# Attention and gated feed-forward on eight cores: f32 products replaced by f16 high and low parts, and two evacuations moved to ScalarE

## The reference, cut to what matters

```python
x = L0_attn_x                                  # (8, 2048, 1024) f32
xn = _layernorm(x, axis=-1)
qkv = einsum('bnd,ed->bne', xn, w_qkv)         # q, k, v of 512 columns each
sim = einsum('bid,bjd->bij', q, k) * 512**-0.5 # causal
s = einsum('bnd,od->bno', softmax(sim) @ v, w_out) + b_out
h = silu(xn @ (w_gate/127).T) * (xn @ (w_up/127).T)   # hidden 3072, weights are int32
g = silu(h @ (w_down/127).T)
return x + s * g
```

## Time and profile before

| | us |
|---|---|
| median of 3 runs | 3124.9 |
| the profiled execution | 3124.2 |
| its span on the slowest core | 3122.6 |
| PE busy | 2814.2 (90%) |
| DVE busy | 223.4 (7%) |
| ACT busy | 216.1 (7%) |
| spans of the eight cores | 3111.6 to 3122.6 |

### The profile page before, as it was taken

How to read it: one execution, slowest core, us unless ns; L and a number is a source line. 1 busy time by engine, 2 the same in 40 slices (tenths; PEclk the granted TensorE clock), 3 DMA queues, 4 the chain that set the end, 5 groups by cost and what they waited for, 6 DMA issues and landing times.

```text
span 3122.6 us, 17440 instructions; the slowest of 8 cores (3111.6 to 3122.6 us)
## 1 busy us (share of the span) xinstructions
PE 2814.2 (90%) x6812; PEld 1313.7 (42%) x6812; DVE 223.4 (7%) x356; ACT 216.1 (7%) x347; POOL 1.9 (0%) x7
## 2 busy tenths in 40 slices
PE   5668998564888899999999999999999999999997
PEld 4555444221434344444444444444444444444443
DVE  1111001000111000000010000001000001000001
ACT  2111001100111100000000000000000000000000
POOL 0000000000000000000000000000000000000000
PEclk9888998876999999999999999999999999999998
DMA  3000002997000032223232223223223223222222
GB/s 96 27 27 0 27 14 61 168 169 147 21 14 21 19 84 79 81 69 127 74 108 81 68 80 121 74 74 108 81 81 107 86 77 108 79 69 81 94 74 101
DMA packets 235905, 240.34 MB, mean 77 GB/s; under 512 B 6129, under 2 KB 211185, under 8 KB 235250
## 3 DMA queue, kind: packets, MB, share of 16 engines
q1 hardware_dynamic: 234674, 199.39, 21.2%
q0 software_dynamic: 624, 37.75, 7.2%
q10 hardware_dynamic: 528, 2.10, 0.2%
HBM read 222.43 MB, written 54.53 MB: 89 GB/s over the span
## 4 chain that ended last, share of the span: by engine, by line
PE 88%; another core or an unknown queue 4%; ACT 3%; issue 2%; DVE 1%; DMA 1%; DVEq 0%; ACTq 0%; SPq 0%
PE psA L246 58%; PE psA L896 11%; PE psB L246 9%; PE psC L896 5%; PE psB L896 5%; ACT oaT L678 1%; ACT xnT L440 1%; ACT xnsc L424 1%; ACT pT L629 0%; ACT oaf L661 0%; DVE st L402 0%; ACTq L959 0%; DVEq L404 0%; DMA xin<-x 0%
## 5 line engine op out<-in xcount | busy, mean ns | idle before, releaser
L246 PE MATMUL psA<-xnT,wgb 128*128 128x512 f32 x1536 | 681.6, 597 | 19.3 <-ACTq L959 10.0
L246 PE MATMUL psA<-xnT,wub 128*128 128x512 f32 x1536 | 674.9, 593 | 0.0
L246 PEld LDWEIGHTS psA<-xnT,wgb 128*128 128x128 f32 x1536 | 294.5, 192 | 391.4 <-issue 391.4
L246 PEld LDWEIGHTS psA<-xnT,wub 128*128 128x128 f32 x1536 | 292.5, 190 | 366.7 <-issue 366.7
L896 PE MATMUL psA<-wdb,hT 128*128 128x512 f32 x768 | 345.5, 593 | 5.7 <-DVEq L959 5.7
L246 PE MATMUL psA<-xnT,wqf 128*128 128x512 f32 x512 | 233.8, 621 | 22.7 <-ACTq L959 17.9
L246 PE MATMUL psB<-vtk,pT 128*128 128x512 f32 x272 | 133.7, 650 | 108.4 <-DVEq L959 96.0
L896 PEld LDWEIGHTS psA<-wdb,hT 128*128 128x128 f32 x768 | 145.9, 190 | 190.4 <-issue 190.4
L246 PE MATMUL psA<-wvf,xnT 128*128 128x256 f32 x512 | 140.6, 444 | 54.1 <-ACTq L959 54.1
L896 PE MATMUL psC<-wdb,hT 128*128 128x512 f32 x384 | 180.5, 592 | 0.0
L896 PE MATMUL psB<-wdb,hT 128*128 128x512 f32 x384 | 180.5, 593 | 0.0
(11 more groups left out here) (57 smaller groups left out, 417.0 us busy)
## 6 DMA issues: line engine op xcount, KB each, us to landing
wgb<-wgb_scr SPq DMA_DIRECT2D x96, 512.0 KB, 3.9
wub<-wub_scr SPq DMA_DIRECT2D x96, 512.0 KB, 5.2
wdb<-wdb_scr SPq DMA_DIRECT2D x96, 512.0 KB, 3.2
xt<-x SPq DMA_DIRECT2D x16, 512.0 KB, 3.5
sscr<-stl SPq DMA_DIRECT2D x16, 512.0 KB, 2.9
sin<-sscr SPq DMA_DIRECT2D x16, 512.0 KB, 7.6
xin<-x SPq DMA_DIRECT2D x16, 512.0 KB, 9.0
out<-otl SPq DMA_DIRECT2D x16, 512.0 KB, 3.5
```

Source lines behind the costliest of these rows:

```text
L246: k.op("te", lambda e, lf=lf, rf=rf, j=j, n=n, pf=psum_ap_fn: e.matmul(pf(), lf(), rf(), start=(j == 0), stop=(j == n - 1)), inc=(inc if j ...
```

## The change

Two things change.

1. `MODE` becomes "split". `xnT`, `qT`, `kT`, the V tiles, `pT`, `oaT` and `hT` are each held as two f16 tiles, high (the rounded value) and low (the rest). The weights of the projections and of the output are multiplied by 64 and split in the same way; the FFN weights are whole numbers up to 127 and need one f16 tile. A product of two split operands becomes three f16 matmuls (high x high, high x low, low x high): projections, scores, PV, output. A product with an FFN weight becomes two. Scratches and buffers of the FFN weights are f16, so POOL's three DMAs write f16 and the loads of wgb, wub and wdb carry 256 KB instead of 512 KB, in pieces of 256 B (gate, up) and 2 KB (down) instead of 512 B and 4 KB. New on DVE: `emit_wv_split` and `emit_wsplit` (multiply, then multiply and subtract), a subtraction behind each evacuation by ACT, and in the FFN three operations per slice (multiply, cast, subtract) instead of one. `wo` is loaded in four parts, each split by ACT and DVE before the next is loaded.

2. `emit_v_group` and `emit_qk_group` evacuate the high part on ACT (`activation`, Identity); DVE then computes the low part. Waits for the bank go by that last writer. The scores also wait for ACT's count at the end of stage 1.

The core of the diff (the V group; the q and k group has the same edit with 512 columns and `dst`, m, n):

```diff
-MODE = "fp32"
+MODE = "split"
...
         if prev is not None:
-            k.wait("te", "ve", prev)
+            k.wait("te", prev[0], prev[1])
...
-        k.wait("ve", "pe", pe_g)
+        k.wait("se", "pe", pe_g)
+        k.op("se", lambda e, tc=tc, hh=hh, bank=bank: e.activation(
+            vtk[0].ap()[:, tc, hh * 256:(hh + 1) * 256],
+            psA.ap()[:, bank * 512: bank * 512 + 256], AF.Identity, bias=zeroc.ap()))
+        k.drain_inc("se", "se")
+        se_c = k.cnt["se"]
         if split:
-            k.op("ve", lambda e, tc=tc, hh=hh, bank=bank: e.tensor_copy(
-                vtk[0].ap()[:, tc, hh * 256:(hh + 1) * 256],
-                psA.ap()[:, bank * 512: bank * 512 + 256]))
-            k.op("ve", lambda e: e.drain())
+            k.wait("ve", "se", se_c)
             k.op("ve", lambda e, tc=tc, hh=hh, bank=bank: e.tensor_tensor(
                 vtk[1].ap()[:, tc, hh * 256:(hh + 1) * 256],
                 psA.ap()[:, bank * 512: bank * 512 + 256],
                 vtk[0].ap()[:, tc, hh * 256:(hh + 1) * 256], ALU.subtract))
+            k.drain_inc("ve", "ve")
+            ve_evac_qk[bank] = ("ve", k.cnt["ve"])
         else:
-            k.op("ve", lambda e, tc=tc, hh=hh, bank=bank: e.tensor_copy(
-                vtk[0].ap()[:, tc, hh * 256:(hh + 1) * 256],
-                psA.ap()[:, bank * 512: bank * 512 + 256]))
-        k.drain_inc("ve", "ve")
-        ve_evac_qk[bank] = k.cnt["ve"]
+            ve_evac_qk[bank] = ("se", se_c)
...
     ve_p1_done = k.cnt["ve"]
+    se_p1_done = k.cnt["se"]
...
             k.wait("te", "ve", ve_p1_done)
+            k.wait("te", "se", se_p1_done)
```

More of the change, by code:

```diff
@@ L376, in emit_qk_group @@
         m = mi % 4
-        k.wait("ve", "pe", pe_g)
+        k.wait("se", "pe", pe_g)
+        k.op("se", lambda e, dst=dst, m=m, n=n, bank=bank: e.activation(
+            dst[0].ap()[:, m, n * 512:(n + 1) * 512],
+            psA.ap()[:, bank * 512:(bank + 1) * 512], AF.Identity, bias=zeroc.ap()))
+        k.drain_inc("se", "se")
+        se_c = k.cnt["se"]
         if split:
[L379 to L382, removed]
+            k.wait("ve", "se", se_c)
             k.op("ve", lambda e, dst=dst, m=m, n=n, bank=bank: e.tensor_tensor(
@@ L386, in emit_qk_group @@
                 dst[0].ap()[:, m, n * 512:(n + 1) * 512], ALU.subtract))
-        else:
[L388 to L392, removed]
+            k.drain_inc("ve", "ve")
+            ve_evac_qk[bank] = ("ve", k.cnt["ve"])
+        else:
+            ve_evac_qk[bank] = ("se", se_c)
     emit_wq_load(0)
```

## The result

The changed kernel takes 2091.1 us (median of 8 runs, 2088.3 to 2093.4) against 3125.9: a ratio of 0.6692, interval 0.6684 to 0.6700. The forecast was 2330 us with a range of 2050 to 2470; the measured time lies in the range, 239 us under the forecast and 16 us under the rival in which the clock stays at 1.00 (2107).

A forecast was written before the change was run, and what follows sets the result against it. PE was taken as the bound, with FFN streams two thirds of the span. At clock 0.81: 3124 - 743 (FFN) + 15 (seams) - 21 (first stage) - 2 (q, k) + 25 (wo) - 66 (attention) = 2332, said 2330 us; range 2050 to 2470.

The forecast's parts named there:

- the rival in which the clock stays at 1.00: FFN products run at full granted clock, 977 us less than before, total 2107 us; chance 0.27.
- What bounds the kernel: Whole kernel: PE is busy all the time in the feed-forward part, whose 4608 records take 1972 us, two thirds of the span.
- The price of a stream: FFN products: an f16 matmul of 512 columns takes 216 ns, so 4608 take 995 us at clock 1.00.
- The clock: FFN: granted clock taken as 0.81, so products take 1229 us, 743 less than now; chance 0.5 at or near 0.81.
- FFN seams: Before down phases and at h=2 of three slabs: new waits, sum +15 us at 0.81, +24 at 1.00.
- Weight feed: FFN weight loads: 4.25 us of DMA a step, landed 5.6 us after release, hidden under the step, so nothing.
- the feed rival: FFN weight loads: each 256 B piece costs as two and sets the step; 2490 us, or 2420 at clock 1.00; chance 0.06.
- First stage: V rounds gain nothing, three rounds with q and k gain 15 us, dense blocks 6: sum -21 us.
- q and k: Slices mi 2 to 7: faster products, but six waits of 4.5 us for the weight split; 166 against 168, -2 us.
- wo: Output weight before attention: four rounds of load, ACT and DVE at 6.5 us each, +25 us.
- Attention: Products -85 us, low-part chains +37, cold clock +16, shorter weight conversion -34: sum -66 us.
- the f16 stream at f32's price: All matmuls: 512 f16 columns take 428 ns like f32, FFN stays 1972 us, kernel about 3570 us; chance 0.02.

The follow-up runs named there:

- the experiment with one pass: Gate and up leave out the pass with the low part of xn, against the changed kernel: 1876.9 us profiled, 1880.9 and 2015.8 in the other two.

## Why the prediction was right where it was, and wrong where it was not

**What bounds the kernel.** Right. PE sets the end through 4608 FFN streams before and after, and the stages with three passes gained little.

**The price of a stream.** Right: 216 ns taken from the V record by equal bytes, 215 measured. That the bytes are the reason is not shown; the number was one row's, and it fitted.

**The clock.** This is the term that was mis-sized, and the step of the forecast that failed: "I take 0.81 for FFN". The runs show 1.00, in the changed kernel and with full-size operands in the place of the low parts and weights. It is a term of 995 / 0.81 - 995 = 234 us, and the forecast missed by 239. The row of 0.81 that it rested on is a mean over full and half clock after pauses of PE: of the same V products 32 took 10.01 us behind a pause and 7.07 without one. So it was a row on idle time, used for a stage that has almost none. The nearest row on dense work was the f32 FFN at 1.00, and the traces spoke for it alone. The rule of the Trainium skill that all-core dense matmul runs at 13/16 of the clock ("TensorE: Matmul & The Clock Gate", Part 1) was not borne out in these stretches: by it a stream would have taken some 265 ns (215 x 16/13, an estimate).

That the range of 2050 to 2470 holds 2091 is owed to its lower end, which was drawn for the full clock, a case given 0.27. The forecast itself stood on the other one.

**FFN seams.** Right in place and size: PE waits 2.7 us ahead of each down phase (10.8 in four) and waited 1.4 before (5.7 in four), so 1.3 more where 1.0 to 1.4 was put, and the new wait at h=2 of a slab, worked out from SP's order as 6 us, measured 6.4. The cast takes 0.43 us, inside its bounds.

**Weight feed.** Hidden, as forecast. Its size was between bytes and pieces, nearer to bytes: 2.5 us of the DMA engines for a step where 4.25 was put, landed after 3.8 us. The 4.25 was read from a stretch with other loads in it; today's megabyte takes 3.8, so both it and the price of the feed rival started too high. wdb landed after 2.6 us, forecast 2.5.

**First stage.** 18 us less, forecast 21. A round's pause of 7.43 us against 7.6.

**q and k.** The six waits were there, 4.0 to 4.2 us against 4.5; the first operation of the split takes 0.69 us instead of 1.2. The experiment that moved the split shows waits and half clock together as 37 us; the forecast had 42. The stage took 9 us less, forecast 2.

**wo.** +23 us against +25.

**Attention.** -81 against -66. The conversion landed after 177.4 us where three quarters of 231.5 gave 174, and DVE's waits behind it fell from 169.5 to 93.2 us. The three tiles behind it took 151 us and take 81 without it, so 70 us were lost where 66 had been worked out, down from an estimated 100. Of the -81 that is 30; with the -85 of the products, 34 us are left for the new chains and the clock behind them, which were put at 53, 16 of them a guess. No run took those apart.

**The rivals.** The full clock is what happened. Its 2107 is 16 us above the measured time: 15 from attention and 7 from q and k, against 3 to 7 the other way in the first stage and FFN. The weight feed fell by the experiment with one pass, the f16 stream at f32's price by the first stretch.

## What to carry to other kernels

A granted clock below full in a stage with pauses told here how often PE stood still, not what it is granted under load. For a stage that stays dense, take the clock from dense rows, and let a rule that the rows contradict be a rival until a trace shows it. When the main stream gets twice as fast, walk through every queue behind a seam (SP's order, DVE's place behind ACT, one large DMA that small ones share the engines with): here four such waits, each visible in an order list or a wait row before the change, held 136 us. Where two engines both touch a result, moving the first half to a free engine bought nothing (it cost 7 us) while the second half released the waiter; where the moved part was the only one, the round's pause fell from 5.97 to 4.22 us.

## What the runs showed of the hardware that was not expected

- One f16 matmul of 512 columns with its weight load every 215 ns at clock 1.00 on eight cores at once, in stretches of 150 us. With full-size operands in place of low parts and whole numbers it was the same in gate and up: 545 to 558 records in 120 us on each of the eight cores.
- f16 weight loads show 100 ns where f32 ones show 192.
- DVE multiplied 1024 f32 elements in SBUF to f16 in 0.69 us and subtracted with a second tensor in 1.23; the one-source operation runs at nearly twice the pace.
- A conversion from int32 to f16 in HBM takes 177.4 us where the one to f32 took 231.5: three quarters, like the sum of bytes read and written (4 + 2 against 4 + 4 per weight).
- Pieces of 256 B cost the DMA engines 2.5 us for half a megabyte where pieces of 512 B cost 3.8 for a whole one: by the byte the shorter pieces were dearer by three tenths, not twice as dear.
